# A four-layer graph network on one core: the next group is turned amid a group's tile products over four PSUM banks, and the scores are copied out ahead of the next-but-one group's norm

## What is computed

```python
h = jnp.maximum(_layernorm(x, axis=-1), 0.0); x = x + SAGE(h)        # layer 0
h = jnp.maximum(_layernorm(x, axis=-1), 0.0); x = x + GAT_4_heads(h) # layer 1, with batch norms and a feed-forward part
h = jnp.maximum(_layernorm(x, axis=-1), 0.0); x = x + GAT_2_heads(h) # layer 2
h = jnp.maximum(_layernorm(x, axis=-1), 0.0); x = x + RELATIONS(h)   # layer 3
```

## Time and profile before

| | |
|---|---|
| median of three runs | 5924.08 us (5915.43, 5924.08, 5924.83) |
| the profiled execution's own time | 5918.01 us |
| its span, first to last instruction | 5916.3 us |
| mean granted TensorE clock | 0.722 of full |
| busy: TensorE, VectorE, ScalarE, GpSimd | 56%, 50%, 32%, 66% |
| scatters of fronts 1 and 2 (L619), busy | 101.0 us in 98 DMAs, mean 1031 ns |

### The profile page before, as it was taken

The page is one execution under the profiler, slowest core; times in us unless marked ns, Lnnn a source line. Parts: engine busy times, 40 slices in busy tenths (PEclk is TensorE's granted clock), DMA queues, the critical chain, the costliest instruction groups (busy, mean ns, idle before and its releaser), DMA issues. The chain is left out here.

```text
span 5916.3 us, 100213 instructions
## 1 busy us (share of the span) xinstructions
PE 3311.7 (56%) x15772; PEld 2786.6 (47%) x15773; DVE 2935.2 (50%) x7620; ACT 1891.2 (32%) x6493; POOL 3914.0 (66%) x4083
## 2 busy tenths in 40 slices
PE   3445555544565535889899894344555563333332
PEld 3444455444555524667777644233444533333331
DVE  4233344434455665788888744344555552222221
ACT  2111111111122204667777653233444441111110
POOL 4777777677777657777776005777777317777776
PEclk8666777766767757999999995566677785555555
DMA  4222222212122123444443211222222134444443
GB/s 122 61 62 63 64 65 66 71 52 53 52 53 53 48 47 87 109 115 116 115 111 106 99 38 38 54 53 53 53 53 53 25 105 131 131 130 132 133 131 108
DMA packets 441904, 474.75 MB, mean 80 GB/s; under 512 B 131954, under 2 KB 337214, under 8 KB 441695
## 3 DMA queue, kind: packets, MB, share of 16 engines
q0 software_dynamic: 130464, 264.37, 18.5%
q1 hardware_dynamic: 184116, 146.31, 8.2%
q10 hardware_dynamic: 127227, 63.09, 3.6%
HBM read 315.46 MB, written 157.97 MB: 80 GB/s over the span
## 5 line engine op out<-in xcount | busy, mean ns | idle before, releaser
L1175 PE MATMUL pa<-arena,weighted 128*128 x4480 | 871.3, 370 | 843.6 <-POOLq L893 510.2
L1175 PEld LDWEIGHTS pa<-arena,weighted 128*128 128x128 f32 x4480 | 803.8, 275 | 899.7 <-issue 899.4
L422 POOL DMA_INDIRECT arena<-y_tab,slot x784 | 739.7, 944 | 442.7 <-ACT slot L514 233.7
L1592 POOL DMA_INDIRECT arena<-t_tab,src_idx x784 | 788.1, 1005 | 283.2 <-issue 225.0
L899 POOL DMA_INDIRECT arena<-h_tab,src_idx x784 | 742.2, 947 | 307.3 <-issue 232.5
L2478 POOL DMA_INDIRECT arena<-t_tab,src_idx x784 | 751.1, 958 | 244.9 <-issue 232.5
L899 POOL DMA_INDIRECT arena<-sage_tab,src_idx x784 | 739.9, 944 | 261.3 <-issue 227.7
L471 DVE TENSOR_TENSOR_SCAN scan_t<-mask,scan_t,pa 128x512 f32<-128x512 bf16 x196 | 250.8, 1280 | 736.8 <-PE pa L495 736.8
L495 PE MATMUL pa<-ident,arena 128*128 128x128 f32 x784 | 218.5, 434 | 603.3 <-DMA arena<-y_tab,slot 603.3
L2716 PE MATMUL pa<-weighted 128*128 128x130 f32 x2240 | 440.2, 377 | 77.7 <-ACT weighted L2798 51.1
L495 PEld LDWEIGHTS pa<-ident,arena 128*128 128x128 f32 x784 | 140.4, 217 | 681.3 <-DMA arena<-y_tab,slot 428.2
(11 more groups left out here) (515 smaller groups left out, 6572.2 us busy)
## 6 DMA issues: line engine op xcount, KB each, us to landing
gat_tab<-out_rows SPq DMA_DIRECT2D x248, 260.0 KB
scan_rows<-out_rows ACTq DMA_DIRECT2D x196, 256.0 KB, 3.7
arena<-t_tab,src_idx POOLq DMA_INDIRECT x1568
mask<-cut_row SPq DMA_DIRECT2D x196, 128.0 KB, 3.1
arena<-h_tab,src_idx POOLq DMA_INDIRECT x784
arena<-sage_tab,src_idx POOLq DMA_INDIRECT x784
y_tab<-arena SPq DMA_DIRECT2D x49, 256.0 KB, 2.3
arena<-y_tab,slot POOLq DMA_INDIRECT x784, 2.8
```

Source lines behind the costliest of these rows:

```text
L422: nc.gpsimd.indirect_dma_start(out=rows(c, t), out_offset=None, in_=table[:, :], in_offset=bass.IndirectOffsetOnAxis(ap=slot[:, c, t:t + 1 ...
L1175: ins = nc.tensor.matmul(pa[:, b * CE:b * CE + RW], hot[b][:, t * P:(t + 1) * P], ring[:, bass.ds(start + t * RW, RW)], start=(t == 0), st ...
L1592: nc.gpsimd.indirect_dma_start(out=rows[:, g % QR * QT + t, :], out_offset=None, in_=t1_tab[:, :], in_offset=bass.IndirectOffsetOnAxis(ap= ...
```

## The change

In fronts 2 and 3 (those with `by_tile`) the turn of the next group and its copy to SBUF move from ahead of a group's products to between the fourth and the fifth tile, and the wide products go round four banks (both halves of `pb` and both of `pd`) in place of two. The waits for a free bank follow. In fronts 1 and 2 (those with `starts`) VectorE copies a group's scores out before it begins the norm of the next group but one; before, it did so after. Front 1 keeps its turns where they are, and front 3 keeps its order on VectorE.

```diff
+            banks = (pb[:, 0:CE], pb[:, CE:2 * CE], pd[:, 0:CE], pd[:, CE:2 * CE])
...
                     def step(i, b, left):
-                        if left > 1:
+                        if left > 1 and starts is None:
                             front(dve, i + 2)
                         dve.wait_ge(group_product.sem, group_product.past(i + 1))
                         post(dve, i, b)
+                        if left > 1 and starts is not None:
+                            front(dve, i + 2)
...
-                    def multiply(i, b):
+                    def multiply(i, b, left):
...
                         for t in range(NG):
                             if by_tile is not None:
+                                if t == 4 and left > 0:
+                                    turn(i + 1)
                                 ws, bias, n, _ = by_tile
 
-                                pe.wait_ge(tile_out.sem, tile_out.by_last_lap(i * NG + (t + 1 if t > 1 else 2 - t)))
-                                to = pb[:, t % 2 * CE:t % 2 * CE + n]
+                                pe.wait_ge(tile_out.sem, tile_out.by_last_lap(i * NG + (max(t, 1) if t < 3 else max(t - 1, 2))))
+                                to = banks[t % 4][:, 0:n]
...
                     def step(i, b, left):
-                        if left > 0:
+                        if left > 0 and by_tile is None:
                             turn(i + 1)
-                        multiply(i, b)
+                        multiply(i, b, left)
...
-                        n, b, buf = by_tile[2], t % 2, t % NS
+                        n, buf = by_tile[2], t % NS
...
-                        nc.scalar.copy(buffers[:, buf * CE:buf * CE + n], pb[:, b * CE:b * CE + n]).then_inc(tile_out.sem, 1)
+                        nc.scalar.copy(buffers[:, buf * CE:buf * CE + n], banks[t % 4][:, 0:n]).then_inc(tile_out.sem, 1)
...
                     def step(i, b, left):
-                        if left > 0:
+                        if left > 0 and by_tile is None:
                             keep(i + 1, 1 - b)
                         if by_tile is not None:
                             for t in range(NG):
+                                if t == 4 and left > 0:
+                                    keep(i + 1, 1 - b)
                                 if t == NG - 2 and left > 1:
                                     scalar_front(act, i + 2)
                                 copy_product(i, t)
```

## The result

The changed kernel takes 5948.59 us, the median of six runs (5946.39 to 5954.35); the kernel before, on the same chip, 5924.45 us. The ratio is 1.0044, with a 95% interval of 1.0034 to 1.0054: 24 us slower, 3.6 us from the 5945 predicted and within the range.

What follows compares the result with a forecast made beforehand. No engine is full, so the order of waits bounds the fronts; 7.5 + 19.5 - 3.0 gives +24 us, 5942 on the profiled execution's 5918.0, and 5945 us with half the median's 6.1 us excess; range 5934 to 5960.

Steps and rivals of the forecast that it cites:

- The chain: Front 1: copy and norm on VectorE, then turn and multiply on TensorE, run in series, 12.0 us a group; +7.5 us.
- The period: Front 2: time from one group's copy of scores to the next grows from 9.6 to 14.1 us.
- The ring: Front 2: late statistics delay ScalarE's norm, the sixth tile copy waits behind it, and TensorE's next group waits for that copy.
- one sum: Front 2: VectorE's new order and the bank and turn edit forecast together at +19.5 us, bounds +17 to +22.
- the first rival: Fronts 1 and 2: the norm stays hidden and GpSimd never starves; -11 us in all, 5907; chance 0.02.
- The start: Front 3: the first tile of group 1 starts at 4777.7 instead of 4782.84, 5.1 us won.
- The ring of 12.7: Front 3: tiles, turn, fifth tile, its copy and ScalarE's norm in series take 12.7 us a group, four times.
- I take the clock as kept: Front 3: TensorE's clock is assumed unchanged, a tile staying at 1.42 us, in the -3.0 us forecast.
- the third sign: Front 3 ends about 3 us sooner from its block's start, at an unchanged clock.
- the sum: Front 3: four rings of 12.7 us and a last step of 12.2, together 63.0 us against 60.9 before.
- the third rival: Front 3: the clock falls to 1.2 GHz, up to 8 us more per ring, up to +64, 5985; chance 0.04.
- the base: Whole kernel: starting time before the change, the profiled execution's 5918.0 us plus half of the median's 6.1 us excess.

Runs made afterwards that it cites:

- e1: Changed kernel with one edit undone: in front 1 VectorE again norms group i + 2 before copying group i's scores; ratio 1.0027, 15.4 us over the kernel before.
- e3: Kernel before with only VectorE's new order in fronts 1 and 2, old banks and old turn; ratio 1.0050, 29.9 us over the kernel before.
- e4: Changed kernel with ScalarE's norm moved behind all seven tile copies of a group in fronts 2 and 3; ratio 1.0018, 11.1 us over the kernel before.
- e8: Changed kernel plus ten unused identity transposes on TensorE ahead of each later group's first tile in front 3; ratio 1.0042, 25.0 us over the kernel before.
- e2: Changed kernel with VectorE's old order in all fronts, leaving only the moved turn and four banks; ratio 0.9998.
- after: The changed kernel itself, all edits together, against the kernel before; 5948.59 us, ratio 1.0044.
- e6: Kernel before with the moved turn and four banks in front 3 alone, fronts 1 and 2 as before; ratio 1.0001.
- e9: Changed kernel with VectorE's old order, ScalarE's norm behind all tile copies in front 2, and ten filler transposes per gap in front 3; 5910.49 us, ratio 0.9987.

## Why the prediction was right, step by step

**Front 1: +9.0, forecast +7.5.** The chain was right in each link. The first copy came 18.7 us from the front's start instead of 21.2, thus 2.5 us earlier (forecast 2.6). The copies stand 12.6, 12.4, 12.4, 12.2 and 11.8 us apart, 12.25 in the mean and not 12.0: copy and norm, forecast at 7.26 us, took 7.78 in the first step (2101.51 to 2109.29) and less in later ones, and TensorE with its handovers about 4.7. Five times 0.25 us, and a first copy 0.1 us later than forecast, are the missing 1.5 to within 0.1. GpSimd waits 15.4 us over five groups, 3.1 each (forecast about 3). e1 shows the cause by taking it away.

**Front 2: +18.1, forecast +19.5.** The first copy came 3.3 us earlier (3.4). The period was 13.8 us and not 14.1, (3675.0 - 3599.6) less the last step of 6.5, by five. Steps at 1.2 GHz throughout took 14.4 us (the first) and 13.85 (the fifth, whose code is written out and not in the loop); the three in which TensorE's clock rose took 13.5 to 13.7. The forecast read the grant of front 2 as 0.50, where the earlier trace rows has 0.52, and asked only whether it could fall. The ring was the forecast one: TensorE idles 6.80 us ahead of a group's first tile until ScalarE's sixth copy. e3 shows that the order of VectorE closes it, e4 that ScalarE's order is its other half. I had put both edits of this front into one sum; the runs show that the bank and turn edit has no share in the loss. In the first rival, the waits of front 2 that would go are 2.5 us and not 2.2; it changes nothing.

**Front 3: +0.9, forecast -3.0.** The start was won as forecast: group 1's first tile came 32.4 us from the front's start (4810.76 - 4778.35), forecast 32.5, where it was 37.6. The ring of 12.7 was right where the clock held (12.7 between the first tiles of groups 2 and 3, 12.4 to 12.7 in e8). The step that failed is "I take the clock as kept", and with it the third sign, an unchanged clock and an end 3 us sooner. It rested on one row, an idle of 1.16 us; the kernel before had others up to 1.63 us without a fall, and the new order's reach 1.90. The idle of 4.52 us ahead of group 1, and what it does to the clock, was not thought of at all. From group 1's first tile to that of group 6 (4877.80) it was 67.0 us where the sum had 63.0, and the 4.0 us are groups 1, 3 and 4 with 1.3 to 1.5 each. So the third rival came true in part, at about 1.4 us a group and not the 8 that I had as its upper end, because the clock is at 1.2 GHz for a part of a group only. e8 shows it from the other side: the same ring with the idle filled is 3.3 us shorter, and at -2.4 us against before close to the forecast. The Trainium skill's "TensorE: Matmul & The Clock Gate", section "A second HAM failure mode: psum-queue depth-cycling", tells of a kernel that cycled through PSUM banks and whose clock swung between its two levels because TensorE idled briefly between groups of matmuls. The traces agree with its direction, with 0.88 of full in those groups.

The forecast's +24 and the medians' 24.1 agree more closely than their terms, and that is luck: front 1 was 1.5 low, front 2 1.4 high and front 3 3.9 low, and the medians lie 3.9 us below the sum of the fronts of the profiled execution. The 3.6 us between 5945 and the result are nearly all the base: I took 5921 for the kernel before, and its median was 5924.45.

**What stays open.** Which idles lower the clock isn't settled; their length alone doesn't decide it. The same code idled 1.91 us and kept the clock in e2 and 1.90 us and lost it in after; in e4 it was kept and lost behind 2.18 us in neighbouring groups. Counted over the profiled executions with the new order in front 3, groups 2 to 5: without the filler (idles of 1.5 to 2.2 us, in after, e1, e2, e4 and e6) the grant fell in 7 of 20, with it (0.5 to 0.8 us, in e8 and e9) in none of 8. That the filler keeps the clock is thus likely, and not proven by so few; a cause that comes and goes by itself, such as the fixed rhythm that e8's expectation names, isn't excluded for the falls. Each kernel has one trace, and after's and e2's, whose code in front 3 is the same, differ by 1.8 us there. Open too is why the medians of after and e1 lie 3 to 4 us below the sums of their fronts; the passes that the change doesn't touch vary by about as much.

## What to carry to other kernels

Before you put a consumer's work (here the scores' copy) ahead of a producer's next item on the same engine, ask who waits for that next item: if the engine behind it does nothing else meanwhile, two times that lay beside each other are now in series, and the period is their sum. More buffers free an engine only if the release of the buffer is not queued behind the very thing that has become late; here one tile copy behind a norm cost 3.4 us a group. Measure a stage from its own start to its own end in several kernels: what a change is worth (here 0.1 to 0.5%) is seen there long before it shows in the total.

## What the runs showed of the hardware

A gap of 1.6 to 2.2 us between groups of matmuls can cost nearly as much again as the gap: in some of the groups behind one the mean grant of the next 14 us was 0.88 instead of 1.00, and TensorE's busy time for the same matmuls rose from 10.8 to 12.5 us. Ten transposes that nobody needs, laid into the gap, took 1.1 us of TensorE's time in a group (11.92 against 10.82); groups 3 and 4, which took 14.2 and 14.0 us in after, took 12.5 and 12.4 in e8.

Longer idles didn't only lower the clock. In front 2 of after TensorE idled 6.3 to 6.8 us ahead of each group, and in three of the five steps the grant rose from 0.50 to 1.00 during the group's sixth tile; in the kernel before, which idled 1.8 to 2.1 us ahead of a turn, it rose in none. The traces don't say why.

A scatter's record is usually 0.98 us, but in front 1 of the kernel before five of the 49 lasted 1.77 to 1.85 us, each started 0.1 to 0.2 us behind the start of a 128x896 operation of VectorE's norm; the changed kernel has one of 1.77. No run isolates the cause. Where GpSimd is the bound, as in front 1 of the kernel before, they lengthen the path; the changed kernel's one stood ahead of a wait, which became 2.19 us where the others were 3.2 to 3.4.
